# Eight sequences, one scan: TensorE's block sums dealt over four slots, Gram blocks loaded a stage earlier, VectorE's merge reordered

## What is computed

```python
def _L3_xattn_ref(X, W_init):      # X (8, 256, 256), W_init (8, 256, 256)
    lr = 1.0 / X.shape[-1]
    def step(W, x_t):
        pre = jnp.einsum('boi,bi->bo', W, x_t)
        y_t = jax.nn.sigmoid(pre)
        dW = jnp.einsum('bo,bi->boi', y_t, x_t) - (y_t ** 2)[..., None] * W
        return (W + lr * dW, y_t)
    _, m_traj = lax.scan(step, W_init, jnp.swapaxes(X, 0, 1))
    return jnp.swapaxes(m_traj, 0, 1)
```

## Time and profile before

| | us |
|---|---|
| median of 3 runs | 2733.89 (2731.76 to 2738.29) |
| the profiled execution | 2743.94 |
| its span | 2742.2 |

### The profile page before, as it was taken

How to read it: one execution, slowest core, us unless ns; L and a number is a source line. 1 busy time by engine, 2 the same in 40 slices (tenths; PEclk the granted TensorE clock), 3 DMA queues, 4 the chain that set the end, 5 groups by cost and what they waited for, 6 DMA issues and landing times. The chain is left out here.

```text
span 2742.2 us, 39081 instructions
## 1 busy us (share of the span) xinstructions
PE 2031.4 (74%) x12230; PEld 1715.1 (63%) x12265; DVE 1472.1 (54%) x4679; ACT 785.6 (29%) x2012; POOL 512.1 (19%) x670
## 2 busy tenths in 40 slices
PE   4178699999999759999999807885910667777445
PEld 3155477777777759999999807883510655566323
DVE  5789755555555421111111155676577538988856
ACT  2111133333333211111111103442463423333155
POOL 3567610000000040000000064340024320000110
PEclk9589899999999779999999958996965785567569
DMA  2100010000000260032132131211000030111100
GB/s 92 32 1 0 14 73 4 8 8 8 8 8 0 89 236 25 23 117 71 69 117 71 47 97 28 43 21 35 0 0 0 0 109 26 36 28 35 26 21 31
DMA packets 133827, 113.56 MB, mean 41 GB/s; under 512 B 60384, under 2 KB 118760, under 8 KB 133736
## 3 DMA queue, kind: packets, MB, share of 16 engines
q1 hardware_dynamic: 120280, 94.67, 11.3%
q10 hardware_dynamic: 10384, 9.45, 1.0%
q0 software_dynamic: 3072, 8.39, 0.9%
HBM read 78.00 MB, written 24.05 MB: 37 GB/s over the span
## 5 line engine op out<-in xcount | busy, mean ns | idle before, releaser
L1481 DVE TENSOR_TENSOR me_h<-me_sg,me_ps_u 128x512 f32<-128x512 f32 x106 | 72.9, 688 | 346.9 <-PE me_ps_u L1412 346.9
L1412 PE MATMUL me_ps_g<-me_xT,me_w 128*128 128x128 f32 x1696 | 208.5, 276 | 12.9 <-DMA me_w<-in_L_ffn_w_s 12.9
L1412 PEld LDWEIGHTS me_ps_g<-me_xT,me_w 128*128 128x128 f32 x1696 | 203.2, 193 | 16.4 <-DMA me_w<-in_L_ffn_w_s 13.3
L1412 PE MATMUL me_ps_u<-me_xT,me_w 128*128 128x128 f32 x1696 | 207.5, 276 | 0.0
L1421 PE MATMUL me_ps_y<-me_w,me_h 128*128 128x256 f32 x848 | 200.6, 379 | 0.0
L1412 PEld LDWEIGHTS me_ps_u<-me_xT,me_w 128*128 128x128 f32 x1696 | 198.8, 193 | 0.0
L989 ACT ACTIVATE ca_e<-ca_main,ca_neg_max 128x256 f32<-128x256 f32 x256 | 119.1, 470 | 211.0 <-DVE ca_neg_max L1037 211.0
L1421 PEld LDWEIGHTS me_ps_y<-me_w,me_h 128*128 128x128 f32 x848 | 152.9, 190 | 16.4
L1461 ACT ACTIVATE me_sg<-me_ps_g 128x512 f32<-128x512 f32 x106 | 63.3, 597 | 337.6 <-PE me_ps_g L1412 337.6
L902 PE MATMUL ca_main<-ca_kT,ca_qT 128*128 128x256 f32 x512 | 135.9, 394 | 4.4 <-DVE carrier L79 3.6
L925 PE MATMUL ca_av<-ca_v,ca_eT 128*128 128x64 f32 x1024 | 131.1, 272 | 8.5 <-DVE ca_eT L1033 8.5
(11 more groups left out here) (420 smaller groups left out, 4755.9 us busy)
## 6 DMA issues: line engine op xcount, KB each, us to landing
me_w<-in_L_ffn_w_e SPq DMA_DIRECT2D x24, 1024.0 KB, 8.7
ss_gb<-scan_g_band SPq DMA_DIRECT2D x15, 512.0 KB, 3.9
me_x_tile<-moe_x_list SPq DMA_DIRECT2D x54, 128.0 KB
moe_y_list<-me_y ACTq DMA_DIRECT2D x53, 128.0 KB
moe_x_list<-mr_zeros SPq DMA_DIRECT2D x1, 5248.0 KB, 23.4
la_vw<-in_ctx SPq DMA_DIRECT2D x24, 128.0 KB, 3.4
x_res<-in_x SPq DMA_DIRECT2D x4, 512.0 KB, 8.0
fa_q<-x_norm SPq DMA_DIRECT2D x8, 256.0 KB, 2.4
```

Source lines behind the costliest of these rows:

```text
L1412: last = nc.tensor.matmul(ps[:, j * P:(j + 1) * P], w13[:, buf, w, kt, f:f + P], xT[:, kt, :], start=(kt == 0), stop=(kt == KD - 1))
L1481: nc.vector.tensor_tensor(h[:, c, :, :].rearrange("p j n -> p (j n)"), sg[:, c, :], ps_u[c][:, :], ALU.mult).then_inc(h_ready[c], 1)
```

## The change

Three things, all in the scan:
1. The Gram blocks of blocks 0 and 1 are loaded in `scan_products`, two DMAs per sequence behind that sequence's band copies, and the stage waits for them at its end. In `scan_steps` TensorE no longer waits for them, and SyncE issues both first bands at once.
2. TensorE's whole sums for a block are dealt over the four slots before it by a table, `QUARTER`. Up to two of them, or in slot 3 the block start (with the wait for its Gram block), stand between the transposes of z and the wait for zT; the others stand behind the group.
3. On VectorE nq of the next token is computed at the end of the token (`square`). At i = 0 the sum of the remaining columns moves behind the product. At i = 2 left is added to adds in place, then comes nq of the next token, then far is added into v.

```diff
@@ scan_products, SyncE
                 sp.dma_start(band[NG - 1, b, :, 0:TG], rows[NG - 1, :, 0:TG]).then_inc(band_out, 16)
+                if b == 0:
+                    sp.wait_ge(gm_clear, 1)
+                for n in range(2):
+                    load_gram(sp, gd, gm, b, n).then_inc(gm_in, 16)
             sp.wait_ge(band_out, 2 * 16 * B)
+            sp.wait_ge(gm_in, 2 * 16 * B)
@@ scan_steps
-    SPLIT = (0, 1, 2)
+    QUARTER = (0, 1, 0, 1, 2, 3, 0, 1, 0, 1, 2, 3, 0, 1, 2, 3)
@@ SyncE
-            load_band(0)
-            load_gm(0)
-            load_band(1)
-            load_gm(1)
-            for k in range(2, NBLK):
-                load_gm(k)
+            load_band(0)
+            load_band(1)
+            for k in range(2, NBLK):
+                for b in range(B):
+                    load_gram(sp, gd, gm, b, k).then_inc(gm_in[k], 16)
                 sp.wait_ge(v_ready, TB * (k - 1) + 1)
                 load_band(k)
@@ VectorE
+            def square(t):
+                yt = y_all[:, :, :, t]
+                dve.wait_ge(y_ready, t + 1)
+                nq_done[t] = step(nc.vector.scalar_tensor_tensor(by_batch(nq[:, t % 2, :]), yt, -LR, yt,
+                                                                 ALU.mult, ALU.mult))
@@ token(t), at i == 2, behind far
-                if old > first:
-                    dve.wait_ge(own, left_done)
-                    rest_done = step(nc.vector.tensor_tensor(v[:, :, t + 1 + first:t + 1 + old],
-                                                             adds[:, t % 2, :, first:old],
-                                                             left[:, t % 2, :, first:old], ALU.add))
...
-                if i == 2 and m < NG - 1:
-                    dve.wait_ge(own, rest_done)
-                    dve.wait_ge(merged, m + 1)
-                    cols = v[:, :, TG * (m + 1):TG * (m + 2)]
-                    step(nc.vector.tensor_tensor(cols, cols, far[:, :, :], ALU.add))
+                    dve.wait_ge(own, left_done)
+                    left_done = step(nc.vector.tensor_tensor(lft[:, :, first:old], lft[:, :, first:old],
+                                                             add[:, :, first:old], ALU.add))
+                    square(t + 1)
+                    dve.wait_ge(merged, m + 1)
+                    dve.wait_ge(own, left_done)
+                    summed[0] = step(nc.vector.tensor_tensor(v[:, :, cols], lft[:, :, first:old], far[:, :, :], ALU.add))
+                    return
@@ token(t), at the end
+                if old > first:
+                    dve.wait_ge(own, left_done)
+                    step(nc.vector.tensor_tensor(v[:, :, cols], add[:, :, first:old], lft[:, :, first:old], ALU.add))
+                if t + 1 < S - 1:
+                    square(t + 1)
@@ TensorE
-            pe.wait_ge(gm_in[0], 16 * B)
             start_block(0)
-            pe.wait_ge(gm_in[1], 16 * B)
             start_block(1)
             for m in range(SENT):
                 k, g = divmod(m, PER)
                 rows = slice(32 * g, 32 * (g + 1))
+                ahead = k + 2 if g >= 2 else k + 1
+                share = [n for n in range(ahead - 1) if (2 if n == ahead - 2 else QUARTER[n]) == (g - 2) % PER]
+                share = share if ahead < NBLK else []
...
                 last.then_inc(z_ps, 1)
+                if g == 2 and ahead < NBLK:
+                    pe.wait_ge(gm_in[ahead], 16 * B)
+                    start_block(ahead)
+                elif g != 2:
+                    for s in share[0:2]:
+                        whole(ahead, s)
                 pe.wait_ge(zT_ready, m + 1)
                 if g < 2:
                     group(k, m, TG * (g + 2)).then_inc(acc_ready, 1)
                 else:
                     group(k + 1, m, 0).then_inc(acc_ready, 1)
-                if k + 1 < NBLK and g < 2:
+                if g < 2 and k + 1 < NBLK:
                     group(k + 1, m, 0)
-                    for s in range(k * (g + 1) // 3, k * (g + 2) // 3):
-                        whole(k + 1, s)
-                if k + 2 < NBLK and g == PER - 1:
-                    pe.wait_ge(gm_in[k + 2], 16 * B)
-                    start_block(k + 2)
-                    for s in range((k + 1) // 3):
-                        whole(k + 2, s)
+                for s in share if g == 2 else share[2:]:
+                    whole(ahead, s)
```

More of the change, by code:

```diff
@@ L2335, in stage_scan, with gram_pair, load_gram @@
         scan_output(nc, core, y_all)
+def gram_pair(n, k):
+    return n * (n + 1) // 2 + k
+def load_gram(sp, gd, gm, b, n):
+    TB = 16
+    rows = gd[b, 0:S * S].rearrange("(k s t) -> s k t", s=TB, t=S)
+    return sp.dma_start(gm[b:P:B, gram_pair(n, 0):gram_pair(n, n) + 1, b, :], rows[:, 0:n + 1, TB * n:TB * (n + 1)])
 def scan_products(nc, core, ins, gd, band, p0, gm, LR, TG):
@@ L2349, in scan_products @@
             "turned", "xT_ready", "cT_ready", "products", "p0_ready", "gs_ready"))
-        band_out, gm_clear = st.sem("band_out"), st.sem("gm_clear")
+        band_out, gm_clear, gm_in = st.sem("band_out"), st.sem("gm_clear"), st.sem("gm_in")
         block = ctx.enter_context(nc.Block())
@@ L2470, in by_batch @@
                 "p (h b) t -> p h b t", b=B)
-        def pair(n, k):
-            return n * (n + 1) // 2 + k
         @block.sync
@@ L2541, in decayed @@
                     out, nq[:, t % 2, :].unsqueeze(2).broadcast_to([P, C, n]), 1.0, src, ALU.add, ALU.mult)
+            nq_done, summed = {}, [0]
+            def square(t):
[3 more added lines that the diff above has]
+                                                                 ALU.mult, ALU.mult))
             def token(t):
@@ L2547, in token @@
                 old = behind if i == 0 else reach
[L2548 to L2560, removed]
+                first = old if i == TG - 1 else 1
+                add, lft = adds[:, t % 2, :, :], left[:, t % 2, :, :]
+                step(product(add[:, :, 0:old], t, i + 1, i + 1 + old))
+                dve.wait_ge(own, max(nq_done[t], summed[0]))
+                left_done = step(decayed(lft[:, :, 0:first], t, v[:, :, t + 1:t + 1 + first], first))
                 if m < NG - 1:
@@ L2569, in token @@
                 dve.wait_ge(own, left_done)
-                nc.vector.tensor_tensor(v[:, :, t + 1:t + 1 + first], adds[:, t % 2, :, 0:first],
-                                        left[:, t % 2, :, 0:first], ALU.add).then_inc(v_ready, 1)
-                if old > first:
-                    left_done = step(decayed(left[:, t % 2, :, first:old], t, v[:, :, t + 1 + first:t + 1 + old],
-                                             old - first))
+                nc.vector.tensor_tensor(v[:, :, t + 1:t + 1 + first], add[:, :, 0:first], lft[:, :, 0:first], ALU.add
+                                        ).then_inc(v_ready, 1)
+                cols = slice(t + 1 + first, t + 1 + old)
                 if i == 2 and m < NG - 1:
@@ L2581, in token @@
                             :, :, :, c0:c0 + TG]
+                    left_done = step(decayed(lft[:, :, first:old], t, v[:, :, cols], old - first))
+                    if m > 0:
                         dve.wait_ge(acc_ready, m)
@@ L2609, in token @@
                                             ).then_inc(z_ready, 1)
+                if old > first:
[3 more added lines that the diff above has]
+                    square(t + 1)
             step(nc.vector.memset(az[:, 1, :, 0:1], 1.0))
             nc.vector.tensor_copy(by_batch(v[:, :, 0:TG]), p0[:, :, :, 0:TG]).then_inc(v_ready, 1)
-            for t in range(S):
+            square(0)
+            for t in range(S - 1):
+                if t % TB == 0:
+                    k = t // TB
+                    dve.wait_ge(gb_in[k % 2], 16 * (k // 2 + 1) + (16 if k == NBLK - 1 else 0))
                 token(t)
@@ L2627, in whole @@
                     nc.tensor.matmul(acc[n % 2][:, h, 0:P], zT[:, k, h, :],
-                                     gm[:, pair(n, k), :, :].rearrange("p b t -> p (b t)"),
+                                     gm[:, gram_pair(n, k), :, :].rearrange("p b t -> p (b t)"),
                                      start=False, stop=True, skip_group_check=True)
@@ L2637, in group @@
                         acc[n % 2][:, h, 0:P].rearrange("p (b t) -> p b t", b=B)[:, :, c0:TB],
-                        zT[rows, k, h, :], gm[rows, pair(n, k), :, c0:TB],
+                        zT[rows, k, h, :], gm[rows, gram_pair(n, k), :, c0:TB],
                         start=False, stop=True, skip_group_check=True)
                 return last
-            pe.wait_ge(gm_in[0], 16 * B)
             start_block(0)
-            pe.wait_ge(gm_in[1], 16 * B)
             start_block(1)
```

4 lines of the change are left out of this document (removed).

## The result

The changed kernel is slower: median 2757.18 us against 2741.22 of the kernel before, run beside it, ratio 1.0052 with a 95% interval of 1.0029 to 1.0074. Beside other kernels on another chip it was 1.0029 (1.0015 to 1.0043). I had forecast 2723 and given slower 0.15.

What follows compares the result with a forecast made beforehand. VectorE and half-speed TensorE were taken to bind by turns. Blocks 1 to 14 -13.4, block 15 -0.5, start and block 0 -1.4 made -15.3 us, cut to -11 from the 2733.89 median: 2723, range 2707 to 2738.

Steps and rivals of the forecast that it cites:

- the switch: TensorE, going from a whole sum to a group's matmuls: between winning 0.17 us and costing 0.3, taken as 0.07.
- no row shows: TensorE: the profile was said to have no row for a whole sum followed by a group, only for the reverse.
- three signs of being wrong: VectorE's z to z stays at 4.34, whole-to-group switch costs 0.3, or blocks 4 to 14 keep one clock level throughout.
- half speed throughout: Rival, TensorE's clock in the scan: level never rises, sums ahead cost more, about 2749 us; chance 0.12.
- the baseline: Scan blocks 1 to 14: 274.2 us before; slow blocks 8 and 10 might be odd, so half of 15.3 taken, -11.
- the stage ahead: Stage before the scan: SyncE's 16 additional DMAs make it end 3.65 us later, bounds 2.5 and 5.
- VectorE's part: VectorE, one full-speed group of the scan: 4.34 us becomes 4.15, a gain of 0.19, bounds 4.10 and 4.30.
- half speed in slots 2 and 3: TensorE's clock in the scan: assumed half speed there, 4.60 us per slot with one sum or block start ahead.
- the clock's level in slots 4 and 1: TensorE's clock: rises around mid slot 4, full in slot 1; block 8 takes 5.3 and 4.15 us there.
- The wash: Rival: switches at 0.3, nq's wait and a 5 us longer stage ahead leave 1 to 4 us, about 2732; chance 0.20.
- Full speed held: Rival, TensorE's clock: blocks 4 to 14 at 16.6 us each, 182.6, a further -23, about 2698; chance 0.08.
- The stall: Start of the scan: VectorE's 4.87 us wait behind both block starts goes; block 0 and the start together -1.4 us.

Runs made afterwards that it cites:

- the preload alone: The kernel before with only Gram blocks 0 and 1 loaded in the stage ahead: ratio to before 0.9998 (0.9977 to 1.0020).

## Why the prediction was wrong

*The step that failed* is the price of a sum or a block start ahead of the group at half speed. I had the mechanism, in the paragraph on TensorE, and the size wrong by 0.37 us per group. The forecast had the transposes' issue at 0.85, then a whole sum at 0.85, the group at 2.1 and far at 3.25, with 0.07 for the switch. Measured: 0.99, 1.16, 2.47 and 3.61. What I called the switch is 0.14 ahead of the sum and 0.31 from its start to the group, 0.45 together, more than the 0.3 that I had as the upper bound. The 0.31 has two parts: the sum's first and second matmul start 0.37 apart where the others are 0.21 apart, and the group's first matmul starts 0.36 behind the sum's last. The row that I took the 0.3 from has the same two parts: in single rows of that timeline the first two matmuls of the sixteen start 0.37 apart (from 2468.38) and the transposes start 0.35 behind the last. So I read "no row shows" where a row did show what follows a whole sum. "The whole-to-group switch costs 0.3" was one of my three signs of being wrong.

With one sum the period is 5.05 instead of 4.60: 0.37 up to far, and 0.08 from far to z, 1.43 where I had 1.35. With a block start it is 5.15 instead of 4.60. With two sums and no work left over from the slot before, at half speed throughout (slot 1 of block 6), it is 5.90 instead of 5.45; slot 4 of blocks 4 to 13 has 5.2 to 6.7, with the level moving in it. Blocks 1 to 3, at one level, show the term clean: 58.0 instead of the 54.9 forecast. In blocks 4 to 14, 220.4 instead of 205.9, it works together with the level.

The forecast, as a ratio, was 0.996 and the measured ones are 1.003 and 1.005, 19 to 25 us apart. The place accounts for about 10 of them; the rest is the baseline, the stage ahead and VectorE's part, below.

The sign of it was there to be read. One sum is 0.85 us and the pause it fills is 0.46, on the chain that binds at half speed. The same section counted half speed in slots 2 and 3, so it had to see that slots with work ahead would cost what the light slots win. I booked the gain to the clock's level in slots 4 and 1 instead. From block 9 on slot 1 did have it, and slot 2 too (4.24 or 4.25 in blocks 9 to 11, where I had 4.15 and 4.60). Slot 4 was a second error. In blocks 4 to 6 its two sums ahead ran at half speed: 2.00 us from the first of them to the group. In blocks 9 to 12 they ran mostly at full speed (1.09 to 1.38 us), but the transposes ahead of them did not, and came late. In block 10, z is at 2487.39 (TensorE, changed kernel; slot 3's sums, then slot 4):

```profile
2485.86 3.78 PE L2645 MATMUL ss_acc<-sc_gm,ss_zT 128*128 128x128 f32 x16
2489.57 1.06 PE L2672 MATMUL ss_ps_z<-ident,ss_z 128*32 128x128 f32 x4
2490.57 1.32 PE L2645 MATMUL ss_acc<-sc_gm,ss_zT 128*128 128x128 f32 x8
2491.81 0.71 PE L2654 MATMUL ss_acc<-sc_gm,ss_zT 32*128 32x128 f32 x4
```

The transposes start 2.18 after z instead of 0.33, behind four sums at half speed. Slot 4 took 6.6 and 6.7 in blocks 10 and 11 where I had 5.9.

*The baseline.* The 274.2 us for blocks 1 to 14 I took from one execution. The order of before gives 264.0 to 280.8. I had noticed the odd blocks and took half of the difference off; against the 264 of two of the traces there was little more than 3 us to win by my own 260.8.

*The Trainium skill's rule* (TensorE: Matmul & The Clock Gate, "What happens when you issue a matmul"), by which a weight load is pulled ahead of running matmuls when its row groups are free or it goes to the background buffer: I had read from it that the switch would be hidden both ways. The trace disagrees with that reading. The first group matmul starts 0.36 behind the last sum's (2294.55 to 2294.91 in single rows of the same timeline), where the matmuls of a sum follow each other by 0.21. The measurement decides. A whole sum takes all 128 rows, so the first of the two conditions is not met here; whether the second is, no run shows.

*Rivals.* The one on the other side, half speed throughout, is right in sign and wrong in mechanism: the level did rise in blocks 4 to 14 (0.58 to 0.87, block 6 alone at 0.50), and their average, 20.04, stayed below the 20.2 from which this rival was to decide. It asked for 2749 by way of slot 3's backlog and two sums at 1.0 each; the place ahead of the group was in it, but the loss did not need its condition. The wash named two costs that came, the switch at 0.3 and the stage ahead 5 us longer, and still left a gain of 1 to 4 us. Full speed held came true only where extra matmuls forced it: blocks 4 to 14 took 193.8 in the changed order and 187.7 and 193.9 with the sums behind, where 182.6 was worked out for it. The Trainium skill's passage on the level that swings with small idle stretches (same page, "A second HAM failure mode") agrees with these two: with the idle stretches filled, the level held at 1.00 over whole blocks. Against it I had set light slots with 2 us of idle time before a fall. Two of the nine falls in the first trace's scan (at 2368.1 and 2388.6) had no idle stretch over 0.8 us around them, so a fall does not need the 2 us.

*VectorE.* Right in direction, half in size: 4.24 instead of 4.34, not 4.15. The timeline of a group at full speed:

```profile
2499.15 0.18 DVE L2621 TENSOR_TENSOR ss_v<-ss_adds,ss_left 128x32 f32<-128x32 f32 x1
2499.31 0.19 DVE L2556 SCALAR_TENSOR_TENSOR ss_nq<-sc_y_all 128x16 f32<-128x16 f32 x1
...
2501.04 0.22 DVE L2593 TENSOR_TENSOR ss_far<-ss_acc,ss_az 128x64 f32<-128x64 f32 x1
2501.18 0.22 DVE L2597 TENSOR_TENSOR ss_left<-ss_left,ss_adds 128x64 f32<-128x64 f32 x1
2501.31 0.18 DVE L2556 SCALAR_TENSOR_TENSOR ss_nq<-sc_y_all 128x16 f32<-128x16 f32 x1
2501.50 0.23 DVE L2602 TENSOR_TENSOR ss_v<-ss_left,ss_far 128x64 f32<-128x64 f32 x1
```

nq of token 1 starts 0.16 after the sum, not 0.11: y's path binds, 0.50 and not 0.48 as I had it. The merge starts 0.32 after left + adds, not 0.26, and 0.19 after nq. In the code two waits stand ahead of it; that the second costs the 0.06 is not shown.

*The start.* The stall went, as told. The stage ahead grew by 4.9 to 5.9 over the 49.3 of before (54.1 to 55.2 in six traces with the preload) instead of by 3.65, mostly just over my upper bound of 5. SyncE's queue was as I had it, 2.82 us per batch where I had 2.75, but it began 0.2 us later, lost 0.76 in one slow issue and 0.4 ahead of another, and its end reads (SyncE's queue, changed kernel)

```profile
2261.68 0.65 SPq L2373 DMA_DIRECT2D scan_g_band<-scan_g  x1
2262.38 1.23 SPq L2347 DMA_DIRECT2D sc_gm<-scan_g  x2
2265.91 0.83 SPq L2494 DMA_DIRECT2D ss_gb<-scan_g_band  x2
```

that is 2.9 us from the last issue (2263.0) to the next stage, where before had 2.72. With block 0's gain it is a trade without profit; the changed kernel's first trace has 5.8 for 4.7, the preload alone 5.4 for 5.2.

What stays open: why the ratio of the changed kernel was 1.0052 on one chip and 1.0029 on another (the intervals overlap), and what sets the moment at which the level rises or falls in one execution.

## What to carry over

Work put into a pause of an in-order engine has to be priced against the pause and not against idle time on average: here 1.16 us, switches included, into a pause of 0.46 us, ahead of the one matmul group that another engine waits for. Price the switches on both sides of what is put in, from single rows. Put filler behind the result that others wait for. And before taking gains from blocks whose length varies from one execution to the next, look at more than one trace.

## What the runs showed of the hardware

More work made this kernel faster: with matmuls whose result nobody reads, TensorE stood at 2.4 GHz over whole blocks (granted clock 1.00 in blocks 8 and 10, where the same order without them had 0.58 and 0.76), and the three kernels with them took 0.7 to 1.0% less time than before. With one TensorE order, five executions differed by 17 us in blocks 1 to 14 (264.0 to 280.8), and the three long ones have a block among 8 to 10 at 0.50 throughout. At half speed, a switch from the last matmul of a sum (128 rows) to the first of a group (32 rows) cost 0.15 us in start-to-start distance (0.36 against 0.21), the start of a whole sum behind the transposes 0.14, and the sum's second matmul came another 0.16 late (0.37 against 0.21).
